# One long kernel of four stages: up products, transposes, block seams and first loads placed elsewhere

## The chip, the cores and the metric

The kernel runs on one core of a Trainium2 chip. The metric is the time on the device in microseconds (us) of one execution; of several executions the median is given. Shares of "faster", "same" and "slower" in this text mean by more than 2% of it, or within.

## What is computed

The input is `x`, four sequences of 1024 rows with 128 features, all in float32. The reference applies, one after the other, six layers with residual sums:

```
x = x + 0.5 * _L0_ffn_ref(_layernorm(x, axis=-1), ...)     # small attention over the batch, then a mixture of experts
x = x + _L0_attn_ref(_layernorm(x, axis=-1), ...)          # hierarchical attention, 16 heads
x = x + 0.5 * _L0_ffn_ref(_layernorm(x, axis=-1), ...)     # the same mixture again
x = x + 0.5 * _L1_ffn_ref(_layernorm(x, axis=-1), ...)     # an MLP with binarised weights
x = x + _L1_attn_ref(_layernorm(x, axis=-1), ...)          # a recurrence over all 1024 rows, then an MLP
x = x + 0.5 * _L1_ffn_ref(_layernorm(x, axis=-1), ...)     # the binarised MLP again
```

The mixture has 8 experts of width 256, two of which count for each row; its attention runs over the four sequences at one position. The hierarchical attention works on blocks of 16 rows at six levels, each level a pairwise pooling of the one before. The recurrence is `state = tanh(state @ A.T + xb_t)` with 32 states, one step for each of the 1024 rows, so the steps depend on each other; the four sequences go side by side in one step.

## The kernel before, in words

The rows are cut into 8 groups of 128 positions, and a group holds these positions of all four sequences, so its tiles are 128 x 512. All x stays in SBUF (`x_all`). Each engine has a program of its own, written out in the order in which it runs, and they meet only at semaphores. A program consists of blocks: at the end of a block every engine waits for all others.

**First block** (`macaron_kernel`). SP issues the loads of x of group 0, of the first weights (`first`: columns, identity, wqkv), of x of group 1 and of the attention's weights (`products`: four of 512 KB and a small one), and waits for the first weights. VectorE sets the tile `att_values` of the attention to zero and writes two constants.

**First mixture stage** (`causal_moe_ffn`). SP first raises each of its semaphores by one (26 of its own and 12 of the second front), then issues the remaining loads (`late_loads`): x of group 2, the expert weights, x of groups 3 to 7, all others. TensorE transposes and projects group 0 (`p_turn1`, `p_qkv`), multiplies the attention's weights with each other (`mn_products`, 32 products, which wait for all five loads of `products`), waits for the expert weights, and then runs group after group: 16 up products and 32 down products, between which stand the small steps of the next two groups. ScalarE copies the banks of `mn_products` (`mn_raw`) ahead of the exponential of group 0 (`a_exp`). VectorE adds an expert's result to x after each pair of down products (`add_expert`).

**Attention stage** (`hierarchical_attention`), one sequence after the other (`entry`). Its head, for sequence 0, is a chain: statistics and normalisation, transposes, ScalarE's copy into `xT` (`rows_out`), GpSimd's pooling of five levels (`pool_levels`, five sums of which each needs the one before, and then the sum of x and the output bias), ScalarE's float16 keys of each level (`hi_keys`), VectorE's rest of each (`lo_keys`), ScalarE's copy `keys_twice`, and TensorE's products with the keys (`xm`) and transposes (`turn_values`). For sequences 1 to 3 the same steps stand among the work of the sequence before. `split_sums` and `all_levels` are VectorE's steps on the softmax's sums, about 70 us into a sequence.

**Last stage** (`ffn_and_recurrence`): the second mixture, the two binarised MLPs ("a" before and "z" after the recurrence) and the recurrence with its MLP ("r"), in ten bodies, g = -1 to 8. A block of its own comes first, in which SP raises the stage's 49 semaphores by one. In body g the 128 steps of the recurrence on group g stand among the other work. TensorE's program is written with an account: after each product `spend(ns)` credits an assumed duration, and when the credit reaches the body's quota, a step is inserted (`step`, with 128-column weights `r_wideA`); in a part marked dense nothing is credited. What is left of the 128 steps follows at the end of the body one by one (`pause(128)`, with 32-column weights `rnnA`):

```
                    if dense[0]:
                        return
                    spent[0] += ns
                    credit[0] += ns
                    if credit[0] >= quota[0] and scanned[0] < limit[0]:
                        step(quota[0] >= 360.0)
                        credit[0] = min(credit[0] - quota[0], quota[0])
```

ScalarE's program takes its tanh of each step from the same account. Body 7 (`LATE`) is the last with steps; its quota is 430. `last_scanned` is its program: transposes, up and down products of "z" for groups 3, 4, 5, 6 and of "r" for group 6, and the mix of group 6 (`p_mix`). An up part is 8 half products of 470 ns by the account, a down part 16 products of 245, a transposing part 4 of 150, the mix 4 x (200 + 245). Body 8 is the rest for group 7.

## Time and profile before

| | us |
|---|---|
| median of 3 runs | 1770.3 |
| the three runs | 1770.04, 1770.3, 1803.4 |
| the profiled execution | 1762.66 |
| its span, from the first to the last instruction | 1760.9 |
| mean granted TensorE clock in it | 0.914 of full |
| TensorE busy | 1534.5 (87%) |
| VectorE busy | 982.5 (56%) |
| ScalarE busy | 825.8 (47%) |
| GpSimd busy | 194.6 (11%) |

A row of the timeline has the start and the length in us, the engine, the line, the operation, what it writes and reads, and in brackets how long the engine had been idle before it and what ended that. PE is TensorE's matmul, PEld its weight load, DVE is VectorE, ACT ScalarE, POOL GpSimd, SPq the issuing of DMAs on SP; L414 is line 414 of the kernel. A matmul in float32 is two instructions, so a step of the recurrence is two. Shares of busy time are means over stages with different limits.

### The profile page before, as it was taken

What the parts mean: (1) busy time and instruction counts of PE and PEld (TensorE: products, weight loads), DVE (VectorE), ACT (ScalarE), POOL (GpSimd) and SP (SyncE); (2) the same over time, 40 slices, a digit from 0 to 9 for tenths busy, and PEclk for the clock granted to TensorE, in tenths of its full rate; (3) what the DMA queues carried; (4) which work ended last, traced back from release to release, by engine and by line L of the source; (5) the groups of instructions that cost most, each with busy time, mean ns of one, the idle gap of its engine ahead of it and who ended that gap; (6) DMA issues with size and microseconds to landing.
All of it is one profiled execution on the core that took longest, in us unless ns stands there. A gap on an engine that the chain in (4) does not pass through costs nothing.

```text
span 1760.9 us, 35102 instructions
## 1 busy us (share of the span) xinstructions
PE 1534.5 (87%) x13496; PEld 1246.0 (71%) x13496; DVE 982.5 (56%) x2976; ACT 825.8 (47%) x2353; POOL 194.6 (11%) x319
## 2 busy tenths in 40 slices
PE   4899899776986996986877989999999999999976
PEld 3576667544955855856766868888888888888865
DVE  5679677468778778687764324444533433223412
ACT  2454454274664664664333424545454544434341
POOL 2212111010100100100321111101111100000100
PEclk8999999887997997997988959999998999899987
DMA  7000000000000000000000000000000000000000
GB/s 198 1 1 1 1 1 2 0 1 2 2 1 2 2 2 2 2 1 2 2 1 1 1 1 1 1 7 1 7 1 1 1 1 1 1 1 1 14 19 6
DMA packets 12071, 13.02 MB, mean 7 GB/s; under 512 B 1712, under 2 KB 10704, under 8 KB 11344
## 3 DMA queue, kind: packets, MB, share of 16 engines
q1 hardware_dynamic: 11904, 10.77, 2.3%
q8 instruction: 107, 1.75, 0.4%
q14 instruction: 60, 0.49, 0.1%
HBM read 8.67 MB, written 2.10 MB: 6 GB/s over the span
## 4 chain that ended last, share of the span: by engine, by line
issue 44%; POOL 3%; POOLq 2%; PE 1%; DVE 0%; DVEq 0%
POOL att_big L747 1%; POOL r_root_p L973 0%; POOL r_root_r L973 0%; POOL r_root_a L973 0%; POOLq L972 0%; POOL r_root_z L973 0%; POOLq L738 0%; POOLq L730 0%; PE r_up L1119 0%; PE r_down L1180 0%; POOL r_roots L965 0%; DVE r_xn_z L1594 0%; POOLq L734 0%; POOLq L964 0%; POOLq L736 0%
## 5 line engine op out<-in xcount | busy, mean ns | idle before, releaser
L1023 PEld LDWEIGHTS r_scan<-r_state,r_wideA 128*128 128x128 f32 x1876 | 302.6, 195 | 94.0 <-ACT r_state L1362 16.0
L1362 ACT ACTIVATE r_state<-r_scan 32x4 f32<-32x4 f32 x1024 | 170.7, 167 | 419.2 <-PE r_scan L1023 401.4
L1023 PE MATMUL r_scan<-r_state,r_wideA 128*128 128x4 f32 x1876 | 303.2, 232 | 6.2 <-ACT r_state L1362 5.4
L1145 PE MATMUL r_down<-moe,r_hT 128*128 128x128 f32 x1024 | 189.9, 301 | 0.0
L1571 DVE SCALAR_TENSOR_TENSOR x_all<-r_down,r_weight,x_all 128x128 f32<-128x128 f32 x256 | 72.1, 344 | 183.9 <-PE r_down L1145 182.8
L1119 PE MATMUL r_up<-r_x2T,moe 128*128 128x256 f32 x512 | 164.6, 426 | 2.6 <-ACT r_hT L1434 2.6
L2358 DVE TENSOR_TENSOR att_big<-at_ring,att_big 128x512 f16<-128x512 f32 x192 | 124.1, 686 | 46.0 <-ACT att_big L2010 45.3
L331 PEld LDWEIGHTS f_down<-moe,f_hT 128*128 128x128 f32 x1024 | 126.1, 195 | 31.3 <-issue 25.7
L1145 PEld LDWEIGHTS r_down<-moe,r_hT 128*128 128x128 f32 x1024 | 142.2, 194 | 1.1
L2010 ACT ACTIVATE att_big<-at_ring 128x512 f16<-128x512 f32 x192 | 111.5, 596 | 65.4 <-PE at_ring L2161 63.2
L331 PE MATMUL f_down<-moe,f_hT 128*128 128x128 f32 x1024 | 127.6, 279 | 3.5 <-ACT f_hT L218 3.5
L322 PE MATMUL f_up<-f_x2T,moe 128*128 128x512 f32 x256 | 122.0, 603 | 5.5 <-ACT f_hT L218 5.5
L2161 PE MATMUL at_ring<-at_keys,att_M 128*128 128x512 f16 x384 | 105.6, 395 | 15.9 <-DVE at_coarse_q L2345 9.2
L533 DVE SCALAR_TENSOR_TENSOR x_all<-f_down,f_weight,x_all 128x128 f32<-128x128 f32 x256 | 71.9, 343 | 69.9 <-PE f_down L331 69.8
L218 ACT ACTIVATE f_hT<-f_up 128x512 f32<-128x512 f32 x128 | 75.3, 597 | 65.8 <-PE f_up L322 64.6
L1434 ACT ACTIVATE r_hT<-r_up 128x256 f32<-128x256 f32 x256 | 91.7, 373 | 10.1 <-PE r_up L1119 10.0
L2458 DVE SCALAR_TENSOR_TENSOR att_big<-at_ring,att_big 128x512 f16<-128x512 f32 x128 | 81.4, 683 | 21.7 <-ACT att_big L2054 21.2
L2254 PE MATMUL at_s<-att_Nhi,att_big 128*128 128x128 f16 x1024 | 91.3, 219 | 0.0
L1119 PEld LDWEIGHTS r_up<-r_x2T,moe 128*128 128x128 f32 x512 | 85.6, 201 | 7.5 <-ACT r_hT L1434 4.3
L2180 PEld LDWEIGHTS at_s<-at_keys,att_big 128*128 128x128 f16 x768 | 63.8, 97 | 38.1 <-DVE att_big L2358 22.5
L2254 PE MATMUL at_s<-att_Nlo,att_big 128*128 128x128 f16 x512 | 87.5, 219 | 0.0
L2180 PE MATMUL at_s<-at_keys,att_big 128*128 128x16 f16 x768 | 71.5, 171 | 18.2 <-DVE att_big L2358 18.2
(343 smaller groups left out, 2978.6 us busy)
## 6 DMA issues: line engine op xcount, KB each, us to landing
x_all<-in_x SPq DMA_DIRECT2D x8, 256.0 KB, 7.5
moe<-in_moe SPq DMA_DIRECT2D x2, 1024.0 KB, 9.9
out<-x_all SPq DMA_DIRECT2D x8, 256.0 KB, 2.3
att_big<-in_att_wq SPq DMA_DIRECT2D x1, 512.0 KB, 6.4
att_big<-in_att_wk SPq DMA_DIRECT2D x1, 512.0 KB, 8.3
att_big<-in_att_wv SPq DMA_DIRECT2D x1, 512.0 KB, 10.2
att_big<-in_att_wo SPq DMA_DIRECT2D x1, 512.0 KB, 11.1
bin<-in_bin SPq DMA_DIRECT2D x2, 256.0 KB, 4.9
```

Source lines behind the costliest of these rows:

```text
L322: nc.tensor.matmul(up[c % UP_RING][:, :], w1[:, c * 128:(c + 1) * 128], x2T[b][:, :], start=True, stop=True).then_inc(s_up, 1)
L331: last = nc.tensor.matmul(down[e % 2][:, s * 128:(s + 1) * 128], hT[c % H_RING][:, s * 128:(s + 1) * 128], w2[:, c * 128:(c + 1) * 128], s ...
L1023: nc.tensor.matmul(at(to, t), weights[:, :], last, start=False, stop=(t == 127), skip_group_check=True).then_inc(s_step, 1)
L1119: ins = nc.tensor.matmul(up[u % 2][:, half], weights, rhs[:, half], start=(j == 0), stop=True, skip_group_check=True)
L1145: ins = nc.tensor.matmul(down[e % 2][:, s * 128:(s + 1) * 128], hT[c % H_RING][:, s * 128:(s + 1) * 128], w2[:, c * 128:(c + 1) * 128], st ...
L1362: nc.scalar.activation(at(state[b][0:STATE, :]), at(scan[b][0:STATE, :]), ACT.Tanh).then_inc(s_tanh, 1)
L1434: nc.scalar.activation(hT[c % H_RING][:, half], up[u % 2][:, half], ACT.Gelu_apprx_tanh).then_inc(s_h, 1)
L2010: nc.scalar.activation(XH[c % 2][:, :, h, :], ring[n % RING][:, :].rearrange("p (q i) -> p q i", i=BLK), ACT.Copy).then_inc(s_xhi, 1)
L2161: last = nc.tensor.matmul(ring[n % RING][:, :], att[w][:, h * D:(h + 1) * D], src(lo), start=(i == 0), stop=(i == 2))
L2180: nc.tensor.matmul(o, lh, keys[:, blk, 0, :], start=True, stop=False)
L2254: last = nc.tensor.matmul(sbk[t % 2][:, 0:D], y[t % 2][:, h, :], att[w][:, h * D:(h + 1) * D], start=(h == 0 and n == 0), stop=(h == HEADS ...
L2358: dve.tensor_tensor(XL[c % 2][:, :, h, :], ring[n % RING][:, :].rearrange("p (q i) -> p q i", i=BLK), XH[c % 2][:, :, h, :], ALU.subtract) ...
```

## The change

1. The memset of `att_values` leaves the first block. It comes in four quarters on VectorE in the last group of the first mixture stage, after each of the first four experts.
2. SP's wait for the first weights becomes a wait of TensorE ahead of its first transposes. The loads of the attention's weights go from the first block to the head of `late_loads`.
3. Five engines share the increments of the last stage's semaphores.
4. In the attention stage VectorE pools the levels of sequence 0. GpSimd adds the bias for sequence 0 once the sums of sequence 0 are split. ScalarE's fine keys wait for the rows, its other keys of sequence 0 for the pooling. A semaphore `s_kfine` stands for the fine low keys, and TensorE's first product waits for it; its wait for the last low keys is at product 32.
5. In `last_scanned` the dense part ends ahead of the first up products, and the transposes of the second late group come after the down products of the first.

```
@@ -278,6 +278,8 @@
+                    if g == 0:
+                        pe.wait_ge(*S["first_loaded"])
                     pe.wait_ge(s_xn1, ONE + g + 1)
@@ -573,6 +575,8 @@
                             binarise()
+                        if g == GROUPS - 1 and e < 4:
+                            dve.memset(att["values"][:, 12 * e:12 * (e + 1), :, :], 0.0)
                         if g == GROUPS - 1 and e == 4:
@@ -941,10 +945,31 @@
         with nc.Block() as block:
             @block.sync
             def _(sp):
-                for s in sems:
+                for s in sems[0::5]:
                     sp.sem_inc(s, ONE)
+            @block.gpsimd
+            def _(pool):
+                for s in sems[1::5]:
+                    pool.sem_inc(s, ONE)
+            @block.scalar
+            def _(act):
+                for s in sems[2::5]:
+                    act.sem_inc(s, ONE)
+            @block.tensor
+            def _(pe):
+                for s in sems[3::5]:
+                    pe.sem_inc(s, ONE)
+            @block.vector
+            def _(dve):
+                for s in sems[4::5]:
+                    dve.sem_inc(s, ONE)
@@ -1302,11 +1327,11 @@
                     p_mix(h)
+                    dense[0] = False
                     p_up("z", later[0])
-                    dense[0] = False
-                    p_turn("z", later[1])
                     p_turn("r", h)
                     p_down("z", later[0], range(FC))
+                    p_turn("z", later[1])
                     p_up("r", h)
@@ -1870,6 +1895,7 @@
         s_xT, s_pool, s_khi, s_klo, s_keys = sem("rows_out"), sem("pooled"), sem("keys_hi"), sem("keys_lo"), sem("keys")
+        s_kfine = sem("keys_lo_fine")
         s_xm, s_xhi, s_xlo = sem("xm"), sem("xm_hi"), sem("xm_lo")
@@ -1948,11 +1974,16 @@
                     last.then_inc(s_pool, 1)
+                    add_bias(s)
+                def add_bias(s):
                     pool.tensor_tensor(xs(s), xs(s), S["att_bias"][:, :, :].broadcast_to([128, GROUPS, D]),
...
                 scales(0)
-                pool_levels(0)
+                pool.wait_ge(s_sums, ONE + 2)
+                add_bias(0)
                 for s in range(1, NB):
@@ -1971,9 +2002,10 @@
                 def hi_keys(s, l):
+                    if l == (1 if s == 0 else 0):
+                        act.wait_ge(s_pool, ONE + s + 1)
                     if l == 0:
-                        act.wait_ge(s_pool, ONE + s + 1)
+                        act.wait_ge(s_xT, ONE + s + 1)
                         act.wait_ge(s_s, ONE + 6 * s)
@@ -2152,6 +2184,8 @@
                     if n == 0:
+                        pe.wait_ge(s_kfine, ONE + s + 1)
+                    if n == 2 * HEADS:
                         pe.wait_ge(s_klo, ONE + s + 1)
@@ -2331,12 +2365,23 @@
+                def first_levels():
+                    dve.wait_ge(s_xT, ONE + 1)
+                    for l in range(1, LEVELS + 1):
+                        v = xT[:, COL0[l - 1]:COL0[l - 1] + COLS[l - 1]].rearrange("p (t o) -> p t o", o=2)
+                        last = dve.tensor_tensor(xT[:, COL0[l]:COL0[l] + COLS[l]], v[:, :, 0], v[:, :, 1], ALU.add)
+                        if l < LEVELS:
+                            dve.drain()
+                    last.then_inc(s_pool, 1)
                 def lo_keys(s, l):
...
                         fine = xT[:, 0:SEQ].rearrange("p (q i) -> p q i", i=BLK)
-                        dve.tensor_tensor(keys[:, 0:FINE, 2, :], fine, keys[:, 0:FINE, 0, :], ALU.subtract)
+                        dve.tensor_tensor(keys[:, 0:FINE, 2, :], fine, keys[:, 0:FINE, 0, :],
+                                          ALU.subtract).then_inc(s_kfine, 1)
                         return
@@ -2555,6 +2600,7 @@
                 norm(0)
+                first_levels()
                 for l in range(LEVELS + 1):
@@ -2598,6 +2644,7 @@
         S["others_loaded"] = s_others, 16 * len(others)
+        S["first_loaded"] = s_first, 16 * len(first)
         att_ctx = ctx.enter_context(ExitStack())
@@ -2609,6 +2656,7 @@
         def late_loads(sp):
+            load_all(sp, products, S["att_w_loaded"])
             load_x(sp, 2)
@@ -2621,13 +2669,9 @@
                 load_x(sp, 1)
-                load_all(sp, products, S["att_w_loaded"])
-                sp.wait_ge(s_first, 16 * len(first))
...
             def _(dve):
-                if True:
-                    dve.memset(att["values"][:, :, :, :], 0.0)
                 dve.memset(S["minus_half"][:, :], -0.5)
```

## Rows read from the trace of the kernel before

**Rows 1.** The page: granted TensorE clock in 40 slices of 44 us.
```profile
PEclk8999999887997997997988959999998999899987
```

**Rows 2.** Timeline of the first 31 us.
```profile
2.07 5.18 DVE L2630 MEMSET att_values<- 128x6144 uint32 x1 [2.07 <-issue]
...
2.70 0.43 SPq L2604 DMA_DIRECT2D x_all<-in_x  x1
...
5.68 0.67 SPq L2609 DMA_DIRECT2D att_own<-in_att_own  x1
...
7.64 0.09 DVE L644 MEMSET f_peak<- 128x32 f32 x1 [0.36 <-PEq L2618]
...
9.79 0.38 SPq L2604 DMA_DIRECT2D x_all<-in_x  x1
...
22.27 2.94 PE L376 MATMUL f_up<-att_big 64*128 64x128 f32 x24
...
30.20 0.41 ACT L197 ACTIVATE f_probs<-f_shifted 128x256 f32<-128x256 f32 x1
```

**Rows 3.** DMA views at 0:1.2 and 0:60: KB each, us to landing.
```profile
x_all<-in_x SPq DMA_DIRECT2D x1, 256.0 KB, 2.8
...
moe<-in_moe SPq DMA_DIRECT2D x2, 1024.0 KB, 9.9
...
att_own<-in_att_own SPq DMA_DIRECT2D x1, 16.0 KB, 11.5
```

**Rows 4.** Timeline, VectorE in the first mixture's last group.
```profile
319.79 1.12 DVE L533 SCALAR_TENSOR_TENSOR x_all<-f_down,f_weight,x_all 128x128 f32<-128x128 f32 x4 [2.38 <-PE f_down L331]
```

**Rows 5.** Timeline of attention's sequence 0; L2339 by its line (min/median/max ns).
```profile
341.93 0.09 DVE L2552 MEMSET at_keys<- 128x32 uint32 x1 [0.84 <-PEq L2636]
...
352.19 3.17 POOL L1947 TENSOR_TENSOR at_xT<-at_xT 128x512 f32<-128x512 f32 x5 [5.03 <-ACTq L1971]
355.32 2.35 POOL L1951 TENSOR_TENSOR x_all<-x_all,att_bias 128x1024 f32<-128x1024 f32 x1
355.39 1.91 ACT L1978 ACTIVATE at_keys<-at_xT 128x2048 f16<-128x2048 f32 x1 [3.38 <-POOL at_xT L1947]
...
360.51 1.47 ACT L2076 ACTIVATE at_keys<-at_keys 128x1520 f16<-128x1520 f16 x1 [1.04 <-DVE at_coarse_q L2345]
...
423.39 0.23 DVE L2392 TENSOR_TENSOR at_sums<-at_sums 128x64 f16<-128x64 f32 x1
...
426.11 1.05 DVE L2404 TENSOR_TENSOR at_xn<-at_xn,at_cden 16x256 f32<-16x256 f32 x2 [1.31 <-ACT at_cden L2024]
...
434.29 0.20 POOL L1936 TENSOR_TENSOR at_root<-at_mv,epsilon 128x8 f32<-128x8 f32 x1 [76.62 <-DVE at_mv L2322]
...
L2339 DVE TENSOR_TENSOR at_keys<-at_xT,at_keys x4: 1215/1216/1417, 357.3 to 724.9; 128x1024 f16<-128x1024 f32 x4
```

**Rows 6.** Timeline, VectorE's first instruction of the last stage.
```profile
878.12 1.03 DVE L1720 MEMSET r_state<- 128x512 f32 x2 [3.31 <-PEq L943]
```

**Rows 7.** Timeline of the last scanned group's body, beginning.
```profile
1633.28 4.03 PE L1119 MATMUL r_up<-r_nT_z,bin 128*128 128x256 f32 x16
...
1639.93 0.55 PE L1053 MATMUL front<-ident,r_xn_z 128*128 128x128 f32 x3 [2.61 <-DVE r_xn_z L1594]
...
1640.95 0.44 PE L1053 MATMUL turn<-ident,r_xn_r 128*128 128x128 f32 x2 [0.19 <-DVE r_xn_r L1594]
...
1644.26 0.69 DVE L1630 TENSOR_TENSOR x_all<-x_all,r_resid 128x512 f32<-128x512 f32 x1
```

**Rows 8.** Stretches: length, then busy us and instructions of PE, PEld, DVE, ACT, POOL, clock.
```profile
1653.19:1658.77 5.58, 5.58 (x33) 4.77 (x33) 0.71 (x3) 4.27 (x16) 0.00 (x0) 1.00 0.01 3
```

**Rows 9.** Groups by line, 1630:1720.3: busy us, mean ns, idle before them.
```profile
L1023 PE MATMUL r_scan<-r_state,r_wideA 128*128 128x4 f32 x168 | 25.6, 223 | 0.1
...
L1023 PE MATMUL r_scan<-r_state,rnnA 128*32 128x4 f32 x88 | 11.6, 202 | 11.3 <-ACT r_state L1362 11.3
```

**Rows 10.** A stretch in the page's 24th slice, as rows 8.
```profile
1022.00:1040.00 18.00, 18.00 (x74) 16.63 (x73) 1.32 (x9) 6.85 (x25) 3.08 (x7) 0.50 0.00 0
```

## Prediction

> **What bounds the kernel now.** I read the page's clock row first [rows 1], then the beginning as a timeline [rows 2] with the DMA view for the landings [rows 3], the last group of the first mixture stage [rows 4], the head of the attention stage [rows 5], the boundary into the last stage [rows 6], and the body of the last scanned group, as a timeline, by stretch and by line [rows 7 to 9]; last a stretch at half clock [rows 10]. The reader is to see that the change leaves the loops alone, in which TensorE is nearly always busy, and works at four places where TensorE is idle because one chain of small operations runs through all engines. At such a place an earlier end of the chain shifts everything behind it. So each place is worth what its last wait is worth, and the four add up, because a semaphore, and no fixed time, starts everything behind each of them.
>
> **The beginning.** The first block holds all engines until VectorE's 5.18 us memset of the value tiles is over; the next block's first VectorE instruction is at 7.64 [rows 2]. With the memset gone, the block ends with SP's fifth issue, which is over at 2.70 + 0.43 = 3.13. From the memset's end (7.25) to 7.64 is 0.4 us, so the next block opens at about 3.5: 4.1 us earlier. Group 0's x is no obstacle: issued at 0.72, it lands after 2.8 us [rows 3], at 3.5. The wait for the first weights goes to TensorE's first transposes, which wait for the normalised rows anyway. Free.
> What is late next are the attention weights. Their five loads leave the first block and follow SP's 38 semaphore increments in the second, which take 9.79 - 7.64 = 2.15 us. The first is then issued at about 5.65 and the fifth, with the same spacing, at 8.15 and not at 5.68: 2.5 us later. The fifth landed 11.5 us after its issue [rows 3], at 17.2; with the same queue ahead of it that becomes 19.7. TensorE's head products, which wait for all five, began at 22.27 right behind the first group's projections, and would be free at 18.2 now. So they start between 18.2 (the queue ahead has thinned, since group 1's x has landed by then) and 19.7 (it hasn't), which wins 4.1 or 2.6 us. ScalarE copies the eight product banks next and only then reaches the exponential at 30.20, which VectorE's value products and all behind them wait for; so this chain and not the scores decides. I take 3.0, near the lower end, since the rows show a full queue: the expert weights too take 9.9 us to land. SP issues them within 3 us of 9.79, so they land by 22.7, and by 25.2 now, still ahead of the exponential at 27.2. The other loads move 2.5 us too; nobody wants them before the third group.
>
> **The memset, moved.** In the last group of the first stage VectorE adds an expert in 1.12 us and then stands idle for 2.38 us [rows 4]; a quarter of 5.18 is 1.3 us. That fits into each of the four gaps, so the price is nothing; without that cover it would be 5.2.
>
> **The head of the attention stage.** Now, one after the other: GpSimd pools the five levels (352.19, 3.17 us), ScalarE writes the fine high keys (355.39, 1.91), VectorE the low keys of all levels (357.3 to 360.5), ScalarE the doubled keys (360.51, 1.47), for which TensorE's first transposes and ScalarE's first copy wait [rows 5]. After the change ScalarE's fine keys need only the rows, so they run from 352.1 to 354.0 beside VectorE's pooling. A VectorE sum over 512 columns takes 0.69 [rows 7]; halving sizes down to 32 columns I estimate at 0.42, 0.28, 0.21 and 0.18, with four drains 2.1 to 2.2 us in all, so the levels are there at 354.3. The low keys then start at 354.35 and not at 357.3: 3.0 us. Their order and sizes stay, and the doubled keys move by the same 3.0. The new semaphore lets TensorE multiply the first fine keys at 355.8, but that product waits in its bank for ScalarE, which stands in the doubled keys; worth nothing more. The wait for the last low keys moves to TensorE's 33rd product, long after they are there. Against the gain: TensorE's clock isn't full here (the page's ninth slice, [rows 1]) and could rise a little later relative to the work (0 to 0.5 us).
> The bias sum leaves GpSimd's queue at 355.32 and comes behind VectorE's second split of the sums, at about 423.6. Nothing is queued behind it before the next statistics, for which GpSimd has been idle 76.62 us at 434.29, and VectorE asks for it only after that. Its 2.35 us end at 426.0, and VectorE's next sum of two SBUF operands starts at 426.11. One row shows what the neighbourhood costs: the fine low keys took 1.417 us at the most and 1.216 in the median of four, and those of the first sequence started, at 357.3, before the bias sum's end at 357.67 [rows 5]. If that is the slow one, 0.2 us are won there. The Trainium skill's page "SBUF — State Buffer" (section "SBUF: two separate sides") says that VectorE and GpSimd share a port pair held as an exclusive lock, against a VectorE operation with two SBUF inputs when GpSimd reads SBUF. By that rule a bias sum that starts 0.3 us later than I think would hold the sum at 426.11 back by about that much; the trace's 0.2 us agrees with the rule, and neither moves my sum. I take 3.0 for this place, between 2.3 and 3.4.
>
> **The boundary into the last stage.** VectorE waits 3.31 us there [rows 6], and 0.84 us at the entrance of the attention stage, which has two block boundaries as well but between them no block that increments semaphores [rows 5]. The difference, 2.47 us, is SP's 49 increments, 0.050 us each (the 38 of rows 2: 0.057 each). Spread over five engines they are ten each, 0.5 us. An increment on the other engines isn't shown; at SP's price 1.95 us are won, at three times that price 1.0, at no price 2.4. I take 1.9.
>
> **The last scanned group.** TensorE inserts a step of the recurrence whenever the credited work exceeds 430 ns, except in dense parts, and runs what is left alone at the end of the body. Following the accounting through the body gives 84 inserted steps and 44 alone, and the rows agree: 168 wide and 88 narrow instructions, two to a step [rows 9]. With the dense part ended before them, the first up products (8 x 470 ns) insert 8 steps, and the remainder carried over makes a ninth in the transposes behind them: 93 and 35. A step alone costs (11.6 + 11.3) / 44 = 0.52 us [rows 9], so 9 x 0.52 = 4.7 us go from the end.
> What they cost: the up products took from 1633.28 to 1637.3 [rows 7], and the same eight with steps between take 5.58 [rows 8]; they end at 1638.9. TensorE was idle for 2.61 us until 1639.93, and then waited for the recurrence's normalised rows until 1640.95, which VectorE delivers at the same time as before. So eight steps lie in idle time, for nothing. The ninth comes after 1640.95 and costs 0.3 to 0.5. The transposes of the second late group lay in that idle time, too; behind the down products they have no cover: four transposes, about 0.7 us with their step. VectorE isn't held up, since it updates x for 2 x 0.69 us before it asks for them. Sum 4.7 - 0.4 - 0.7 = 3.6, between 2.8 and 4.7. The products of the final group behind it keep their order.
>
> **Sum.** 3.0 + 3.0 + 1.9 + 3.6 = 11.5 us. The profiled execution took 1762.66 (span 1760.9): 1751.2 for such a one. The three runs have a median of 1770.3, 7.6 above it, and I forecast against that: 1758.8. The bounds of the terms add to 8.7 and 14.6: 1755.7 to 1761.6. A measurement of this kernel tells about 2%, 35 us, from no change, so this is inside.
>
> **Rivals.**
> (a) The weights take the whole gain of the beginning: the queue is so full that a load issued 2.5 us later, after an idle spell of the DMA engines, lands over 6 us later. For it: 11.5 us to land 16 KB. Against it: fewer bytes ahead. Then 1770.3 - 8.5 = 1761.8. With the last scanned group's steps also only displaced (the nine steps' tanh delay the activations, so that up products wait), 1765.4; the stretch of rows 8, in which each product carries a step and never waits, speaks against it.
> (b) The clock gets better by chance. In the page's 24th slice, 1012 to 1056, it stands at 5 tenths [rows 1], though TensorE was busy in all 18 us of one stretch of it [rows 10]. At full clock that stretch would take about half, 9 us, and the rest of the slice, with its gaps, perhaps 3 less: 12 us. If the new alignment ends the episode at its start, they are won: 1747.
> The Trainium skill's page "TensorE: Matmul & The Clock Gate" (section "The HAM clock gate") says that the chip's activity window runs freely and doesn't start with the kernel, so that the place of a transition varies. By that rule (b) and (c) are open in every run; no row of one execution can show it.
> (c) Slower: one more such episode. The page's 31st and 35th slices show 8 tenths, which is half clock for up to 2 x 0.2 x 44 = 18 us in each [rows 1]. If it stays down there for a whole slice, as in the 24th, the price is up to 12 us: 1771 with one and 1783 with both. It decides when the half rate lasts about 40 us at one further place.
> (d) The change doesn't shorten the boundaries at all, because a block's end and not the increments is what costs: 1.9 less, 1760.7, inside the forecast.
>
> **Chances.** The forecast with (d) 0.57, its own range 1755 to 1763; (a) 0.15, to 1766; (b) 0.10; (c) 0.12; nothing gained for a reason I don't see 0.06. The range reaches from 1749 to 1769: it takes in the forecast, (a), what loses the gain in part, and leaves out most of (b) and of (c). Faster by over 2% 0.02, slower by over 2% 0.02, else 0.96.
>
> **What would show it.** In the changed kernel: VectorE's first statistics near 4.0; the head products near 19; the expert weights landed by 25. Four memsets of 1.3 us in the last group with TensorE's pace unchanged. From the end of the rows' copy (352.19 at the latest) to the doubled keys 5.3 us where there are 8.3. VectorE's wait at the last boundary 1.4 us. In the last scanned body 186 wide and 70 narrow instructions, and 18.2 us of steps alone and not 22.9. The prediction would be wrong if the weights land after 21, if TensorE waits inside the first up products of that body, or if the sum of half-clock time changes by more than 20 us.

## Result, and the profile after

The changed kernel took 1758.73 us (median of 6 runs, 1757.82 to 1763.17 and one of 1792.67); the kernel before, beside it, 1770.17 (1769.40 to 1771.00 and one of 1803.40). The ratio is 0.9936, with a 95% interval from 0.9926 to 0.9947. That is 11.3 us less and inside 2%. The profiled execution of the changed kernel is the one of 1792.67 us (span 1790.9, clock 0.889); up to 1637 us its rows are like those of the later traces, and what happens behind that turned out to be the main finding.

The page's clock row of the changed kernel, to be laid beside [rows 1]:

```profile
PEclk8999999796997987988799779999999999897567
```

The last four slices are at 7, 5, 6 and 7 tenths, where the kernel before had 9, 9, 8 and 7.

The beginning, timeline of the changed kernel, against [rows 2]:

```profile
3.62 0.09 DVE L648 MEMSET f_peak<- 128x32 f32 x1 [2.73 <-PEq L2666]
...
5.77 0.55 SPq L2656 DMA_DIRECT2D att_big<-in_att_wq  x1
...
8.27 0.59 SPq L2656 DMA_DIRECT2D att_own<-in_att_own  x1
...
18.64 2.94 PE L378 MATMUL f_up<-att_big 64*128 64x128 f32 x24 [0.43 <-DMA att_own<-in_att_own]
...
26.58 0.41 ACT L197 ACTIVATE f_probs<-f_shifted 128x256 f32<-128x256 f32 x1
```

The block opens at 3.62 where it did at 7.64, the last product weights are asked for at 8.27, and TensorE waits for them, but only for 0.43 us. The exponential comes 3.62 us earlier.

VectorE in the last group of the first mixture, against [rows 4], and the head of the attention stage, against [rows 5]:

```profile
313.61 1.34 DVE L579 MEMSET att_values<- 128x1536 uint32 x1 [0.27 <-DVE x_all L535]
315.72 1.13 DVE L535 SCALAR_TENSOR_TENSOR x_all<-f_down,f_weight,x_all 128x128 f32<-128x128 f32 x4 [0.77 <-PE f_down L333]
...
348.49 1.87 DVE L2373 TENSOR_TENSOR at_xT<-at_xT 128x512 f32<-128x512 f32 x4 [2.81 <-ACTq L2002]
...
351.09 1.23 DVE L2383 TENSOR_TENSOR at_keys<-at_xT,at_keys 128x1024 f16<-128x1024 f32 x1
...
354.07 1.47 ACT L2108 ACTIVATE at_keys<-at_keys 128x1520 f16<-128x1520 f16 x1 [0.78 <-DVE at_coarse_q L2390]
...
418.18 2.34 POOL L1980 TENSOR_TENSOR x_all<-x_all,att_bias 128x1024 f32<-128x1024 f32 x1 [74.67 <-DVE at_sums L2437]
...
420.67 1.38 DVE L2449 TENSOR_TENSOR at_xn<-at_xn,at_cden 16x256 f32<-16x256 f32 x3 [1.39 <-ACT at_cden L2056]
...
872.69 1.03 DVE L1745 MEMSET r_state<- 128x512 f32 x2 [2.15 <-PEq L947]
```

Each quarter of the memset lies in VectorE's idle time, of which at least 0.77 us are left. The fine low keys take 1.23 us and not 1.42. The bias sum is over 0.15 us before VectorE's next sum of two SBUF operands. The last row answers to [rows 6]: the wait is 2.15 us where it was 3.31.

The stretch in which the time was lost (length, then busy us of the engines, clock last but two):

```profile
1637.80:1722.90 85.10, 85.10 (x347) 79.40 (x346) 14.34 (x38) 22.29 (x101) 2.42 (x4) 0.50 0.03 10
```

For 85 us TensorE is busy without a break and its clock is at 0.50, the lower level (1.2 GHz). In the whole execution 397 us are at half clock, where the profiled execution of the kernel before has 305.

### The profile page after: what moved, and what is told of

Its sections match the earlier page's. It is cut to its first block, busy times and chain, and to the rows that moved or that the text cites. A ratio compares the mean times of both kernels' runs of the same rounds, so it can differ in the third digit from the quotient of the medians.

```text
span 1790.9 us, 35109 instructions
## 1 busy us (share of the span) xinstructions
PE 1575.1 (88%) x13496; PEld 1284.9 (72%) x13496; DVE 984.7 (55%) x2984; ACT 825.6 (46%) x2353; POOL 191.8 (11%) x314
## 4 chain that ended last, share of the span: by engine, by line
issue 45%; POOL 3%; POOLq 2%; PE 1%; DVE 0%; DVEq 0%
POOL att_big L751 1%; POOL r_root_p L998 0%; POOL r_root_a L998 0%; POOL r_root_r L998 0%; POOLq L997 0%; POOL r_root_z L998 0%; POOLq L742 0%; POOLq L734 0%; PE r_up L1144 0%; PE r_down L1205 0%; POOL r_roots L990 0%; DVE r_xn_z L1619 0%; POOLq L738 0%; POOLq L989 0%; POOLq L740 0%
## 5 line engine op out<-in xcount | busy, mean ns | idle before, releaser
L1048 PEld LDWEIGHTS r_scan<-r_state,r_wideA 128*128 128x128 f32 x1894 | 325.5, 206 | 96.4 <-ACT r_state L1387 15.6
L1048 PE MATMUL r_scan<-r_state,r_wideA 128*128 128x4 f32 x1894 | 315.3, 237 | 6.0 <-ACT r_state L1387 5.4
L2195 PE MATMUL at_ring<-at_keys,att_M 128*128 128x512 f16 x384 | 106.8, 399 | 11.3 <-DVE at_keys L2383 4.6
```

What stands on the lines that cost most here:

```text
L1048: nc.tensor.matmul(at(to, t), weights[:, :], last, start=False, stop=(t == 127), skip_group_check=True).then_inc(s_step, 1)
L2195: last = nc.tensor.matmul(ring[n % RING][:, :], att[w][:, h * D:(h + 1) * D], src(lo), start=(i == 0), stop=(i == 2))
```

## Experiments

The kernels were measured in three groups of four, each group beside the kernel before and on a chip of its own: e1 to e4, e5 to e8, e9 to e12. Beside totals I use a ledger: the start of the same GpSimd instruction in the trace of the kernel before, minus its start in the other kernel's trace. A positive number is a lead in us; a term of the sum is a step from one row to the next. A "fall" is a stretch in which TensorE's granted clock is at half, and "filled" means that transposes of the identity stand in TensorE's idle time in the last scanned body.

| at, in the kernel before | changed (e1) | old start (e2) | old head (e3) | old boundary (e4) | filled (e5) | filled, old order (e6) | before, filled (e7) | changed, other chip (e9) |
|---|---|---|---|---|---|---|---|---|
| 60.2, first mixture | 4.90 | -0.52 | 3.22 | 3.13 | 4.83 | 3.41 | 1.80 | 2.30 |
| 344.7, attention begins | 3.71 | -0.57 | 2.40 | 2.23 | 3.74 | 2.57 | 1.67 | 0.95 |
| 434.3, its second sequence | 5.08 | 2.65 | 1.23 | 2.42 | 5.12 | 2.81 | 0.98 | 3.81 |
| 838.7, ahead of the boundary | 4.22 | 2.68 | -0.11 | 3.12 | 4.32 | 3.51 | 0.64 | 4.61 |
| 884.2, behind it | 5.32 | 3.76 | 0.69 | 3.15 | 5.42 | 4.62 | 0.66 | 5.69 |
| 1594.7, ahead of the last scanned body | 3.31 | 5.72 | 0.93 | 5.94 | 3.41 | 2.58 | 3.49 | 7.62 |
| 1667.4, inside it | -16.75 | -13.91 | -7.14 | -13.24 | 2.35 | 2.56 | 3.48 | -11.90 |
| 1726.2, behind the steps alone | -19.90 | -15.39 | -2.42 | -32.86 | 6.94 | 2.60 | 3.42 | -31.50 |

**e1, the changed kernel again.** No edit.

> The changed kernel once more, unaltered, for a profile whose late part can be read. My terms: first statistics near 4.0, head products near 18.6, the last add of the first mixture stage 3.0 to 3.7 us earlier than in the kernel before, the doubled keys 6 to 6.5 us earlier, the first VectorE instruction of the last stage 7.5 to 8 us earlier, and 3 to 4 us more won in the last scanned body; time 1757 to 1761. Rival (the clock decides): the leads at these landmarks jump by several us between two of them, where the granted clock of the two traces differs, and the time scatters with them.

1784.24 us (1782.55 to 1800.13), where the kernel before had 6 runs of 1765.0 to 1766.8 and 11 of 1798.2 to 1805.7. So the rival of this text was right: the leads jump, and the forecast of 1757 to 1761 failed. At 1637 the kernel was 3.3 us ahead; then it lost 20 us in 30.

```profile
1635.28 0.28 PE L1048 MATMUL r_scan<-r_state,r_wideA 128*128 128x4 f32 x2
1637.65 0.33 PE L1078 MATMUL turn<-ident,r_xn_r 128*128 128x128 f32 x1 [2.09 <-DVE r_xn_r L1619]
```

```profile
1638.60:1699.90 61.30, 61.30 (x249) 57.52 (x249) 12.18 (x35) 15.57 (x71) 2.41 (x4) 0.50 0.03 9
```

Timeline and then a stretch: 2.09 us of idle time of TensorE behind the first up products, and from 0.9 us after its end 61 us at half clock, without a gap. The same stretch of the kernel before is at 1.00 throughout in its one trace, although its idle time there is 2.61 us [rows 7].

**e2, the old beginning.**

```
             def late_loads(sp):
-                load_all(sp, products, ...)
...
+                load_all(sp, products, ...)          # first block
+                sp.wait_ge(s_first, ...)
+                dve.memset(att["values"][:, :, :, :], 0.0)
-                if g == GROUPS - 1 and e < 4: dve.memset(quarter)
```

> The changed kernel with the beginning of the one before (memset and product loads in the first block). My theory: the head products stand at 22.3 again, every landmark up to the end is 3.0 to 3.6 us later than in the changed kernel, time 3 to 3.6 us above it. Rival, that the lead is given back in the first mixture stage because the loops are set by TensorE's work and a later wait: the last add of that stage would be less than 1 us later, and the time the same within 1 us.

The exponential is at 30.55 here, 0.35 us later than in the kernel before, and 3.5 to 3.7 us earlier than there in e1, e3 and e4: the beginning is worth 3.6 us at this place. What is kept of it is less certain. At 60.2 and 344.7 this kernel leads by -0.5 and -0.6 us and e1, e3 and e4 by 3.1 to 4.9 and 2.2 to 3.7, but the trace of the same changed kernel in e9 leads by 2.3 and 0.95 only, and e7, which has the old beginning, by 1.8 and 1.7. The pieces at half clock between 27 and 60 us lie differently in each. The time was 1784.50, as much as e1: both fell to half clock in the last scanned body (58 us of it here), which hides 3.6 us. The totals of this group can't tell 3 us.

**e3, the old head of attention.**

```
-                pool.wait_ge(s_sums, ONE + 2)
-                add_bias(0)
+                pool_levels(0)
-                first_levels()
```

> The changed kernel with the attention head of the one before (levels pooled by GpSimd before ScalarE's fine keys, bias sum right behind). My theory: from the end of the rows' copy to the doubled keys 8.3 us again and not 5.5, fine low keys 1.42 us and not 1.22, the end 3 us later. Rival: TensorE's clock is low in this stage and the stage is set by TensorE or VectorE work further on, so that only the first chunk starts earlier; then the start of the second sequence's first product moves less than 1 us and the time with it.

The doubled keys start at 358.09 and not at 354.00; 1.31 of these 4.09 us were there at the stage's beginning (2.40 against 3.71), so the head is worth 2.8 us. Against the kernel before, the step from the beginning of the stage to the doubled keys is 6.51 - 3.71 = 2.8 in e1, 2.58 + 0.57 = 3.15 in e2, and 0.0 in e3. The fine low keys, by their line (min/median/max ns), in e3 and in e1:

```profile
L2378 DVE TENSOR_TENSOR at_keys<-at_xT,at_keys x4: 1212/1214/1415, 354.9 to 724.8; 128x1024 f16<-128x1024 f32 x4
```

```profile
L2383 DVE TENSOR_TENSOR at_keys<-at_xT,at_keys x4: 1212/1216/1226, 351.0 to 720.6; 128x1024 f16<-128x1024 f32 x4
```

The slow one of four is the one beside the bias sum (352.91 to 355.26), and it is gone with it. By the next sequence e1 had only 1.37 us of its 2.8 left: between 382 and 385 us of the kernel before, the lead fell from 7.04 to 5.63, in a piece at half clock from 375.6 to 379.0, which neither e2 nor the kernel before has there. The change isn't what brings that piece: e7, with the old head, has it too. e2 kept its 3.2 (2.65 + 0.57), e4 and e6 only 0.2; kernels with the old head lost 1.2 (e3) and 0.7 (e7) over the same sequence. e3's total of 1765.77 says nothing on the head: its clock fell for 17 us only in the last body (two stretches, columns as before):

```profile
1639.40:1656.40 17.00, 16.69 (x74) 16.24 (x75) 6.47 (x16) 3.06 (x16) 0.73 (x2) 0.50 0.06 17
1656.50:1690.00 33.50, 33.37 (x235) 29.58 (x233) 6.73 (x21) 16.61 (x72) 1.58 (x3) 1.00 0.03 9
```

Here the clock came back among up products with a step behind each, with no transposes added. One of the twelve runs took 1796.53, the others 1763.22 to 1766.55.

**e4, the old boundary.**

```
-                for s in sems[0::5]: sp.sem_inc(s, ONE)      # and four more engines
+                for s in sems: sp.sem_inc(s, ONE)
```

> The changed kernel with all 49 increments ahead of the last stage on SyncE again. My term: VectorE's last work of attention to its first of the last stage 3.3 us and not 1.4 (the first trace of the changed kernel shows 2.15 us there, which would leave 1.15 us of the 1.9). If the increments are what costs, 3.3; if the block's ends cost, 2.2 as now. The end follows by the same amount.

VectorE's wait is back at 3.31 us, and the step in the ledger is 0.03 where e1, e2, e5, e6 and e9 have 1.08 to 1.11 and e3 has 0.80:

```profile
874.96 1.02 DVE L1725 MEMSET r_state<- 128x512 f32 x2 [3.31 <-PEq L947]
```

So the increments are the price, and the term is 1.1 us, not 1.9. The trace's records of the semaphore instructions tell why: behind the block's opening SyncE makes one each 0.058 us, ScalarE 0.067, GpSimd 0.078, VectorE 0.093, TensorE 0.150. TensorE's nine are over at 872.26 in e5, when the others have been waiting for 0.65 us and more. The stage has 45 semaphores and not 49: the kernel before shows 45 increments here, 2.6 us of them. The total of 1796.89 us can't be read for this term, since the clock fell for 133 us in the last body.

**e5 to e7, TensorE's idle time filled.** In the changed kernel, in the changed kernel with the old order of its last scanned group, and in the kernel before:

```
                     dense[0] = False
                     p_up("z", later[0])
+                    for i in range(16):      # 20 in e6 and e7
+                        nc.tensor.transpose(front[...], ident[:, :], ident[:, :])
                     p_turn("r", h)
```

> The changed kernel with 16 transposes of the identity (into a free bank, results unused) behind the first up products of the last scanned body, where TensorE otherwise stands idle for 2.1 us. In the first profiles of the changed kernel TensorE's clock fell to half at 1638.6, in that idle time, and stayed there for 61 and 85 us though TensorE was busy again. Theory A (the idle time is what lets the clock fall there): no fall near 1638, the last body's rate full, time 1755 to 1762 and less scatter. Theory B (the steps among the products are what lets it fall, at any point of this body): half clock for 20 to 80 us there all the same, time 1770 to 1785.

> The last scanned group's order of the kernel before, all other parts of the change kept, with 20 transposes of the identity in the idle 2.6 us there. If the clock stays full in both, the difference to the filled changed kernel is the order of the last scanned group alone: my term says 3.6 us more here, 44 steps alone and 22.9 us for them where the changed order has 35 and 18.3. Rival (the steps are only displaced): less than 1 us more.

> The kernel before with the same 20 transposes in its idle 2.6 us. If the clock stays full in the last body of both, the filled changed kernel against this one is the whole change without that fall: my sum says 11.5 us, the leads that the traces show up to 1637 (3.3 to 4.4 us) with the last group's 3.6 say 7 to 8. Against the kernel before itself: no run near 1803, all near 1763 to 1766. If the fall comes all the same, some runs stay near 1803.

e5 took 1756.89 us (1751.64 to 1757.35), e6 1759.44 (1755.80 to 1761.50), e7 1763.26 (1758.97 to 1764.95); the kernel before on that chip 1765.17 (23 runs, 1762.03 to 1772.03), never near 1800. Up to 1635 e5's trace is that of e1 within 0.1 us, the pieces at half clock included; and then:

```profile
1635.33 1.94 PE L1333 MATMUL front<-ident 128*128 128x128 f32 x16
1637.56 0.33 PE L1078 MATMUL turn<-ident,r_xn_r 128*128 128x128 f32 x1 [0.29 <-DVE r_xn_r L1621]
```

```profile
1634.80:1694.80 60.00, 59.57 (x431) 53.20 (x430) 16.67 (x47) 27.25 (x121) 2.94 (x5) 1.00 0.05 14
```

The transposes cost nothing (those of the scanned group start 0.09 us earlier than in e1), and the clock stays at 1.00 (2.4 GHz). Now the last body can be read. TensorE's steps alone in e5 and in e6, by shape (busy us, mean ns | idle before them):

```profile
L1048 PE MATMUL r_scan<-r_state,rnnA 128*32 128x4 f32 x70 | 9.3, 204 | 9.0 <-ACT r_state L1389 9.0
```

```profile
L1048 PE MATMUL r_scan<-r_state,rnnA 128*32 128x4 f32 x88 | 11.7, 203 | 11.3 <-ACT r_state L1389 11.3
```

70 narrow instructions against 88, 18.3 us against 23.0. e5 first loses 1.06 us (3.41 to 2.35) and then wins 4.59 (to 6.94); e6 wins 0.02. The order of the last scanned group is worth 3.5 us. The medians are 2.6 apart, 0.9 less than that. The rival of displaced steps falls.

e7's text asked for the whole change without a fall, e5 against e7: 11.5 by my sum, 7 to 8 by the leads up to 1637. It is 6.4 us by the medians (1763.26 and 1756.89). The 23 runs of the kernel before on this chip stand in two clusters, 13 at 1762.0 to 1765.2 with a mean clock of 0.913 to 0.914 and 10 at 1769.3 to 1772.0 with 0.909 to 0.910; e5 is 6 us below the first and 13 below the second. Filled, it has none of its 12 runs in the upper cluster (e7: 1764.95 at the most).

**e8, the attention weights asked for at once.** e5, with the 38 increments of the second block made by TensorE:

```
-                for s in sems + S["second_front"].sems: sp.sem_inc(s, ONE)
                 late_loads(sp)
...
+                for s in sems + S["second_front"].sems: pe.sem_inc(s, ONE)
```

> The filled changed kernel in which TensorE, idle until 11.7, makes the 38 increments of the second block, so that SyncE issues the attention weights at once and not 2.15 us later. If the weights' landing is what TensorE's head products wait for (0.43 us in the trace of the changed kernel), these begin at 18.2 and not at 18.64, and the start is 0.4 us earlier; the first profile shows 5.77 us for the first weight issue, here 3.6. If the queue decides, nothing moves. The end: the same within 1 us.

```profile
3.54 0.55 SPq L2658 DMA_DIRECT2D att_big<-in_att_wq  x1
...
18.04 2.94 PE L378 MATMUL f_up<-att_big 64*128 64x128 f32 x24
```

The products start at 18.04 and not at 18.59, and so does the exponential (25.98, 26.53): the 0.5 us was the landing. 1753.42 us (1750.70 to 1755.86), 3.5 below e5; its text had said the same within 1 us. In its trace the attention stage has fewer pieces at half clock than in e5 (none near 376 and 503), and it leads e5 by 3.6 us at 838.7, so that is not all its own.

**e9, the changed kernel once more,** no edit, on another chip.

> The changed kernel unaltered, beside the filled ones on one chip. Theory A (TensorE's clock can fall in the idle 2.1 us of the last scanned body and then stays low for tens of us): where it falls, 1780 to 1800, where it doesn't 1757 to 1760; nothing between.

1803.70 us: one run of 1756.17, the others 1795.15 to 1805.31. The kernel before: 11 runs, all 1799.21 to 1808.00. Nothing between. The clock falls at 1634.7, 1.4 us behind the same idle time, for 133 us. The ledger goes from 7.65 to -36.0 in the first 98 of them (at 1697.0 of the kernel before). Of these 43.7 us 1.1 are what the new order costs there in e5 too, so a us at half clock cost 0.43 us. The other 35 lie mostly among the steps alone, which it hardly delays (0.53 us each and not 0.48). Timeline and stretch:

```profile
1633.31 0.33 PE L1078 MATMUL turn<-ident,r_xn_r 128*128 128x128 f32 x1 [2.09 <-DVE r_xn_r L1619]
```

```profile
1634.80:1694.80 60.00, 60.00 (x244) 56.31 (x243) 11.64 (x35) 15.35 (x69) 2.41 (x4) 0.50 0.03 9
```

These 60 us hold 244 of TensorE's instructions; the same stretch of e5 holds 431.

**e10, filled, and no increments for TensorE.** SyncE makes 14, GpSimd 11, ScalarE 12, VectorE the other 8 (its text says 12, from a count of 49):

```
-                for s in sems[3::5]: pe.sem_inc(s, ONE)
```

> The filled changed kernel in which TensorE makes none of the 49 increments ahead of the last stage (SyncE 14, GpSimd 11, ScalarE 12, VectorE 12). The trace of the filled kernel shows TensorE's nine increments 0.15 us apart and VectorE's 0.093: TensorE ends last, at 872.37, and VectorE would end at 871.9 with twelve. If the slowest engine's increments are the price, VectorE's wait there falls from 2.15 to 1.7 us and the lead grows from 1.1 to 1.5 us. If the two block ends are, 2.15 stays. No fall of the clock near 1638.

```profile
872.84 1.02 DVE L1742 MEMSET r_state<- 128x512 f32 x2 [1.56 <-PEq L947]
```

VectorE waits 1.56 us, 0.6 to 0.7 less than in the traces of the changed kernel (2.15 to 2.24), and the step in the ledger is 1.65 (3.53 to 5.18). The slowest engine's increments were the price. 1755.24 us (1746.47 to 1756.70), on the chip where the kernel before takes 1802.50: a ratio of 0.9718 (0.9693 to 0.9743).

**e11, everything filled.** e10 and e8's loads, and

```
                     for _ in range(...):
                         step(False)
+                        filler(fill)         # one transpose, last scanned group only
...
+                        filler(20)           # ahead of p_turn("r", h), and of p_turn("z", of) after it
```

> As the one with the new boundary, and further: TensorE makes the second block's increments so that the attention weights are issued at once (0.4 us in the first look at it); one transpose of the identity behind each of the 35 steps alone, and 20 in each of the two idle times of 4.8 us behind them. Theory A carried on (idle and nearly empty stretches let the clock fall, and what follows pays): no half clock from 1695 on, steps alone 0.49 us each and not 0.53 (1.5 us), the last mixing 1.8 and not 3.4 us (1.6), the two last rounds of up products 4.1 and not 5.8 us each (3.4): 6 to 7 us less, near 1749. Rival (the transposes get in the way of the steps or of the work behind them, or the clock falls all the same): 0 to 3 us more than without them.

1753.92 us (1741.96 to 1757.26), ratio 0.9707 (0.9678 to 0.9736): not to be told from e10, where 6 to 7 us less were hoped for. The clock fell all the same while steps alone ran, and then the transposes were in the way: a step took 0.60 us (1698.56 to 1699.16) where e10 has 0.53.

```profile
1698.56 0.27 PE L1043 MATMUL r_scan<-r_state,rnnA 128*32 128x4 f32 x2
1698.75 0.48 PE L1064 MATMUL front<-ident 128*128 128x128 f32 x1
1699.16 0.27 PE L1043 MATMUL r_scan<-r_state,rnnA 128*32 128x4 f32 x2
...
1727.38 1.99 PE L1145 MATMUL r_up<-r_nT_r,mlp 128*128 128x256 f32 x8 [0.90 <-DVE r_nT_r L1634]
...
1741.80 5.90 PE L1145 MATMUL r_up<-r_nT_z,bin 128*128 128x256 f32 x16 [0.78 <-DVE r_nT_z L1637]
```

In the ledger e11 wins 2.2 us over the steps alone where e10 wins 4.6, and has that back later, since the first of the two last rounds of up products takes 4.2 us and not 5.9 (the clock was back at full when the 20 transposes ahead of it ended). In front of the second, 2.6 of its 4.8 idle us had stayed empty, and it runs at half clock still.

**e12, the transposes where TensorE isn't idle.** The changed kernel, with the 16 behind p_down("z", later[0]).

> The same 16 transposes, but behind the down products of the first late group, where TensorE isn't idle: the 2.1 us stay empty. Theory A: the clock falls as often as in the changed kernel beside it, 1782 to 1802, or 1.8 us above its other runs. Rival (any extra work in this body, wherever it is, keeps the clock up or merely shifts the alignment): no fall, 1759 to 1761.

1768.29 us (1763.06 to 1770.81): neither. The trace has both halves of the answer:

```profile
1643.78 0.33 PE L1078 MATMUL turn<-ident,r_xn_r 128*128 128x128 f32 x1 [2.09 <-DVE r_xn_r L1621]
...
1655.54 3.25 PE L1335 MATMUL front<-ident 128*128 128x128 f32 x16
```

```profile
1644.70:1658.30 13.60, 13.60 (x66) 13.60 (x66) 4.23 (x6) 1.77 (x11) 0.00 (x0) 0.50 0.03 10
1658.30:1690.00 31.70, 31.56 (x219) 27.90 (x218) 7.99 (x29) 16.02 (x68) 2.42 (x4) 1.00 0.05 13
```

The idle time stayed, and the clock fell behind it, at 1644.7. It came back at 1658.3, 2.8 us into the 16 transposes, after 13.6 us and not 61 to 133. That the transposes ended it isn't shown: in e3 it came back after 17 us without any. In e1 and e9 TensorE was as busy, with a step of 4 columns behind each product or two, and stayed at half clock. The total isn't all the fall's either: this trace was 2.8 us behind the kernel before at 1594.7 already, where e1 led by 3.3.

The traces together settle the place. All seven with the changed order and nothing in that idle time (the first, e1 to e4, e9, e12) have a fall there, between 0.3 us before the end of the 1.8 to 2.1 us of idle time and 1.5 us behind it, for 85, 61, 58, 17, 133, 133 and 14 us. None of the six filled ones (e5 to e8, e10, e11) has, and e5 differs from e1 in nothing else. The idle time doesn't bring a long fall in every execution: five runs of the first measurement (1757.82 to 1763.17) and one of e9 (1756.17) have the same idle time, and by their times no long fall.

## Why the prediction was right, and where it wasn't

The time was forecast at 1758.8 and is 1758.73. So close a hit is luck in part, as the sum below shows. The terms, each read where it acts:

- **Beginning, 3.0 (2.6 to 4.1).** 3.6 at the exponential, against [rows 2]; 2.8 to 3.8 in all traces with the new beginning. The weights landed at 18.6 and not at the 19.7 of the full queue; I had chosen by the wrong end. TensorE waited 0.4 us for them, so rival (a) falls. The increments took 2.15 us as read. The block opened 0.1 us later than forecast.
- **Memset, nothing.** Right: 1.34 us in gaps of 2.38 [rows 4].
- **Head of attention, 3.0 (2.3 to 3.4).** 2.8 in two traces and 3.15 in one. The levels took 2.13 us in e2, in e1 with a stop of 0.43 us at the last. The 0.2 us at the fine low keys are won, as the shared lock of the Trainium skill's page "SBUF — State Buffer" (section "SBUF: two separate sides") has it: 1415 ns with the bias sum beside it, 1226 at the most without. The bias sum had 0.15 us to spare, as forecast.
- **Boundary, 1.9 (1.0 to 2.4).** Mis-sized: 1.1. The step that failed is "at SP's price": an increment costs 0.058 us on SyncE and 0.150 on TensorE, and the slowest engine holds all. My bound of "three times that price 1.0" was the case. The increments are 45 and not 49, nine for each engine. Rival (d) falls by e4.
- **Last scanned group, 3.6 (2.8 to 4.7).** 3.5, with both parts right: 4.6 won in the steps alone (forecast 4.7), 1.06 paid before (0.4 + 0.7). The instructions are 186 and 70, as counted.

The sum of what was measured at the four places is 3.6 + 2.8 + 1.1 + 3.5 = 11.0 against 11.5. But that terms add up "because a semaphore, and no fixed time, starts everything behind each of them" failed as a statement on one execution: e5, with all of the change, leads by 6.94 at 1726.2 and not by 11.0. 1.4 us went in the first sequence, at the piece of half clock near 376, 0.8 in the other three, and 2.0 between 884.2 and 1594.7, of which 0.8 at about 1525, where its clock fell for 17 us and that of the kernel before twice for 7. How much of that is chance one trace can't tell. Over that same stretch, which no edit touches, the leads of the twelve later traces move by anything from -5.4 (e12) to +2.8 us (e4, e7), and e7, the kernel before with an edit that acts only behind 1637, led it by 1.8 at 60.2 and by 3.5 at 1594.7.

The totals speak for less than 11 us as well. Without falls in the last body the whole change is worth 6.4 us (e5 against e7) or 6 (e5 against the lower cluster of the kernel before), and the order of the last scanned group accounts for 2.6 to 3.5 of it. The ratios of 0.9936 here and 0.9938 (0.9914 to 0.9962) for e5 both give 11 us, because runs of the kernel before at 1770 are in them: 10 of 23 there, and all five here beside the one of 1803.40, while its profiled execution took 1762.66. I forecast against 1770.3. The upper cluster's clock, lower by 0.004 to 0.005, is some 16 us more at half clock, which at 0.43 us each is 7 us, an estimate from these runs. A fall of 17 us in the last body, as e3 has, would do that, and the filled kernel never stands there; but no run at 1770 has a profile. So several of the 11 us may be the clock's, for which my sum had no term. Each of the four steps is shown where it acts. That they are kept to the end in full is not shown.

**What the prediction had wrong** beside this is rival (c), in place and price. I looked at the 31st and 35th slices and priced an episode at up to 12 us. The one that happens begins right at the idle time that follows the first up products of the last scanned body, which in the last scanned group's term I had booked as free cover. It cost 26.8 us with 61 at half clock (e1 against e5 at 1726.2) and 43 to 48 with 133 (43.7 - 1.1 in e9's ledger by 1697.0; its median is 47.5 above its one run of 1756.17). My own sign of being wrong, over 20 us more of half-clock time, came true by 92 us in the profiled execution of the first measurement (397 against 305), and doesn't show in its other five runs (mean clock 0.908 to 0.911). There it struck once in six runs of either kernel; on another chip in 11 of 17 of the kernel before, in all six of the changed one, and at its full price in one of twelve of e3 (group of e1); on a third in 11 of 11 and 5 of 6 (group of e9). I take every time from 1782 up as such a run; of those of the kernel before none has a profile, and that theirs is the same fall is inferred from their mean clock of 0.886 to 0.891 and the 38 us. In the filled kernels it struck in none of 47 runs (e5 to e8, e10, e11). Of these the 11 on the chip of e9 count for most; the other 36 were on one where the kernel before didn't fall so far either, in 23 runs. The forecast of 1758.8 is thus a forecast for executions without the fall, and the 1758.73 is a median of such. On another chip the same change measured 1784.24.

The Trainium skill's page "TensorE: Matmul & The Clock Gate" (section "The HAM clock gate") says that the activity measurement runs freely and that idle time lets the clock fall. The traces agree that it does: 1.8 to 2.1 us of idle time went with a fall in all seven unfilled traces of the changed order, and none came in the six filled ones; but 2.61 us in the kernel before had none behind it. It says also that the default is the low clock and that sustained work releases it. Here 60 us of TensorE 100% busy (e9) did not.

**Open.** Whether the change makes the fall likelier: its idle time is shorter (2.09 against 2.61), but the up products ahead of it are now mixed with steps. The counts per chip (11 of 17 and 6 of 6; 11 of 11 and 5 of 6) don't decide it. Why some chips show it almost always and one never, and what ends it after 17 us in one kernel and 133 in another, are open too. So is the piece of 44 us at half clock that begins at 1007 to 1015 in all traces. No idle time over 0.4 us precedes it, but it begins, as the later one near 1697 does, while steps run alone with 0.26 us of idle time in each 0.48.

## What to carry to other kernels

Before booking an idle time of TensorE as free cover, see what its clock does behind it: 2 us of idle time ahead of a stretch of products and 4-column steps cost 27 to 48 us, and 16 transposes of the identity into a bank nobody reads prevented that for nothing. That was worth 2.7% where the fall is common (1755.24 against 1803.70, with 0.6 us of it from the boundary). Where terms are 1 to 4 us and the clock scatters by 7 to 48, judge each term by the lead at the next instruction behind it in two traces, with a control that leaves the term out. Then don't take the sum of such leads for the gain of the whole: here 11.0 us at four places were 6 to 7 at the end. And see which cluster the runs of the baseline stand in before adding a sum to their median. Give semaphore increments to the engines by their price, and none to TensorE where it is the last.

## What the runs showed of the hardware

- A run of increments costs 0.058 us each on SyncE, 0.067 on ScalarE, 0.078 on GpSimd, 0.093 on VectorE and 0.150 on TensorE.
- With products and 4-column steps in turn, TensorE busy throughout, half clock lasted 17, 58, 61, 85 and twice 133 us (in the last, the steps alone included). In e12 it ended 2.8 us into a run of 16 transposes, in e3 without one.
- 16 or 20 transposes in 2 to 2.6 us of idle time kept the clock full behind it in six traces of six; without them it fell in seven of eight, the kernel before being the eighth.
- A us at half clock costs 0.43 to 0.44 us in this body (e9, e1), and 1.4 us for 3.4 (0.41) in the attention stage.
- One transpose in each gap of the steps alone (0.26 us idle of 0.53; e11) doesn't hold the clock up, and at half clock lengthens the step to 0.60 us.
